# Hadamard stage of a fused kernel: feature groups paired on GpSimd, transform products half as wide, another order of copies

## The chip, the cores and the metric

The kernel runs on one core of one Trainium2 chip. The metric is device time in microseconds (us) of that core, the median of some runs; lower is better. The core has five engines with queues of their own, which run apart from each other and meet only at semaphores: TensorE (PE in the rows, its weight loads PEld), VectorE (DVE), ScalarE (ACT), GpSimd (POOL) and SyncE (SP).

## What is computed

Four layers follow each other on 1024 tokens of 256 features: a token-routed expert layer, a mixture of 16 experts, a latent attention and a ternary feed-forward layer. The change touches only the last one, which is cut here to what matters:

```
def h_bitlinear(x, w):
    return jnp.einsum('bsh,oh->bso', act_quant(fwht(x)), weight_quant(w))
gate = bitlinear(x, w_gate)          # 1024 features out
up = bitlinear(x, w_up)
intermediate = jax.nn.silu(gate) * up
return h_bitlinear(intermediate, w_down)

def act_quant(x, bits=8):            # per token
    scale = 128 / clip(max(abs(x)), 1e-5)
    return clip(round(x * scale), -128, 127) / scale
```

`fwht` is the Walsh-Hadamard transform over the 1024 features of a token. A feature number is a chunk number of three bits (8 chunks of 128) and a place in the chunk; the transform is the 128-point transform within each chunk, and then sums and differences of chunks, one bit of the chunk number at a time.

## The kernel before

The program is written engine by engine; the order on each engine is the order of the code, and there is no scheduler. The last layer works with **units**: unit v (0 to 15) is one chunk of features (v mod 8) of one half of the tokens (v // 8), a block of 128 features by 512 tokens. For each unit:

- TensorE, `products(v)` (L1460 to L1479): four matmuls of bf16, two for gate and two for up, into two of the PSUM banks 0 to 5.
- VectorE, `gate_b(v)` (L2162): gate times the tokens' scale, into `gt`.
- ScalarE, `silu_b(v)` (L999): silu of `gt` into `gsl`.
- VectorE, `up_b(v)` (L2170): `gsl` times up into `hp`, two buffers.
- ScalarE, `hi_b(v)`: a copy of `hp` rounded to fp32r, the high part, into `hpB_hi` or `hpA_hi` (B for the first half of the tokens, A for the second). The line is that of the helper `copy`, L700.
- GpSimd (L689): `hp` minus the high part, the low part, into `hpB_lo` or `hpA_lo`.

Ten units (`AHEAD`) run ahead of the transform. Units 0 to 3 lie beside the end of the attention, which also gives the last two token tiles: their variance goes to GpSimd for the power -0.5 (`power3`, L542), VectorE normalises and quantises them (`quantise`, L1591 and L2137 to L2146), TensorE turns them (L1079, L1458) and ScalarE copies them (`bits_x`, L993). Units 6 and 7 stand behind the turns, units 8 to 15 behind the copies.

Then eight **tiles** t of 128 tokens:

- TensorE, `transform(t)` (L1521): for each of two banks, 4 and 5, four matmuls with the high parts of four chunks and four with the low parts, each 512 columns wide. The moving operand `had` is the 128-point matrix four times side by side with signs, so that the sums over two bits of the chunk number are made in PSUM.
- ScalarE, `f_copy(t)` (L700, `f`): bank 5 into `f1`. VectorE, `butterfly(t)` (L2219, two instructions): bank 4 plus and minus `f1` into `F`, the third bit.
- VectorE, `feature_scale(t)` (L2225 to L2229): maximum and scale. ScalarE, `f_round(t)` (L1040). VectorE, `clip(t)` (L2233).
- TensorE, `turn_f(t)` (L1079, `F`): eight transposes into banks 6 and 7. ScalarE, `f_bits(t)` (L1048): two copies to `fqT`.
- TensorE, `final(t)` (L1545): eight matmuls. VectorE, `x4(t)` (L2237, L2239): the result added to `X`. SyncE stores it.

`transform(0)` to `transform(3)` need all of units 0 to 7, `transform(4)` to `transform(7)` all of units 8 to 15. Units 10 to 15 are made between the first tiles, two for each tile. `turn_f(1)` and `turn_f(2)` also wait for `x4(0)` and `x4(1)`, as `final(0)` and `final(1)` use bank 6.

Of the kernel before, what the change touches and what calls it, by code (L numbers as in the profile page):

```python
# [7 lines left out]
F32 = mybir.dt.float32  # L8
# [68 lines left out]
def build(nc, x_d, tok_d, seg_d, ctxT_d, router_d, gu_d, dn_d, kvc_d, dq_d, uq_d, uk_d, uv_d, qr_d, qrs_d,  # L77
# [6 lines left out]
    with ctx:  # L84
# [9 lines left out]
        def place(words, *groups):  # L94
# [3 lines left out]
            for n, group in enumerate(groups):  # L98
                scope = ExitStack()
                with scope:  # L100
                    for name, (shape, dt) in group.items():
# [96 lines left out]
                        "gt": ([P, 2, BANK], F32), "gsl": ([P, 2, BANK], F32), "hp": ([P, 2, BANK], F32),  # L198
                        "had": ([P, 4, 4, P], F32R), "f1": ([P, 2, BANK], F32), "F": ([P, 2, FI], F32)}))
# [38 lines left out]
        xqT, invB, diag, gt, gsl, hp, had, f1, F = [m[k] for k in "xqT invB diag gt gsl hp had f1 F".split()]  # L238
# [66 lines left out]
        (signs_a, x_scaled_v, x_rounded, xq_turned_p, xq_copied_a, diagonal_v, bit_scaled_v,  # L305
# [3 lines left out]
             "signs_a x_scaled_v x_rounded xq_turned_p xq_copied_a diagonal_v bit_scaled_v "  # L309
# [74 lines left out]
        def x_bank(t):  # L384

            return t % 2 if t < NT - TB else 6 + t % 2

# [151 lines left out]
        def _(pool):  # L539
# [144 lines left out]
            for v in range(2 * NF):  # L684
                if v == BESIDE - 1:
                    power3(NT - TB, TB)
                pool.wait_ge(hidden_high_a, UNITS + v + 1)
                n, c = divmod(v, NF)
                pool.tensor_tensor(hp_lo[n][:, c, :], hp[:, v % 2, :], hp_hi[n][:, c, :].bitcast(F32), ALU.subtract  # L689
                                   ).then_inc(bit_low_g, 1)  # L690
# [3 lines left out]
        def _(act):  # L694
# [286 lines left out]
            def signs():  # L981

                act.wait_ge(masked_v, 4 * PAIRS)
                for r in range(4):
                    for q in range(4):
                        e = act.activation(had[:, r, q, :], had1, ACT.Copy, scale=-1.0 if odd(r & q) else 1.0)
                e.then_inc(signs_a, 1)
# [9 lines left out]
            def silu_b(v):  # L997
                act.wait_ge(bit_scaled_v, v + 1)
                act.activation(gsl[:, v % 2, :], gt[:, v % 2, :], ACT.Silu, scale=bscale[:, 0:1]).then_inc(gate_silu_a, 1)  # L999

            def hi_b(v):
                n, c = divmod(v, NF)
                act.wait_ge(hidden_v, UNITS + v + 1)
                copy(hp_hi[n][:, c, :], hp[:, v % 2, :]).then_inc(hidden_high_a, 1)

            for i in range(SLOTS):
# [19 lines left out]
                if i == PAIRS + 4:  # L1026
                    for v in range(1, BESIDE):
                        silu_b(v)
                        hi_b(v - 1)


            def f_copy(t):
# [3 lines left out]
                copy(f1[:, t % 2, :], bank[5][:, :]).then_inc(transform_copied_a, 1)  # L1036
# [15 lines left out]
            for v in range(BESIDE, AHEAD):  # L1052
# [3 lines left out]
                hi_b(v - 1)  # L1056
# [3 lines left out]
            hi_b(AHEAD - 1)  # L1060
# [15 lines left out]
        def _(pe):  # L1076
# [383 lines left out]
            def products(v):  # L1460
                n, c = divmod(v, NF)
# [9 lines left out]
                for g in range(2):  # L1471
                    if before is not None:
                        pe.wait_ge((bit_scaled_v, hidden_v)[g], (0, UNITS)[g] + before + 1)
                    for k in range(KD):
                        w = slice(k * FI + c * P, k * FI + (c + 1) * P)
# [35 lines left out]
            def transform(t):  # L1511
                n, x = divmod(t, NT // 2)
                tile = slice(x * P, (x + 1) * P)
                for part, ready in ((hp_hi[n], hidden_high_a), (hp_lo[n], bit_low_g)):
                    pe.wait_ge(ready, (UNITS if ready is hidden_high_a else 0) + NF * (n + 1))
                    for z in range(2):
                        if t >= 1 and ready is hidden_high_a:
                            pe.wait_ge((butterfly_v, transform_copied_a)[z], (2 * t, t)[z])
                        for r in range(4):
                            m_ = had[:, r, :, :].rearrange("p q j -> p (q j)")  # L1520
# [841 lines left out]
```

## Time and profile before

| | us |
|---|---|
| median of 3 runs (579.54 to 583.58) | 580.24 |
| the profiled execution | 580.38 |
| its span (first to last event in the trace) | 578.6 |

The page gives the busy time over the span: TensorE 86%, VectorE 79%, ScalarE 61%, GpSimd 55%. The last layer's part of the span is its last 85 us, from about 494 us on; what lies before is the same in both kernels but for the names of a few lines. The profiled execution stands 0.14 us over the median, so its times may be used as they are; 1.78 us of it lie outside the span.

### The profile page before, as it was taken

What the parts mean: (1) busy time and instruction counts of PE and PEld (TensorE: products, weight loads), DVE (VectorE), ACT (ScalarE), POOL (GpSimd) and SP (SyncE); (2) the same over time, 40 slices, a digit from 0 to 9 for tenths busy, and PEclk for the clock granted to TensorE, in tenths of its full rate; (3) what the DMA queues carried; (4) which work ended last, traced back from release to release, by engine and by line L of the source; (5) the groups of instructions that cost most, each with busy time, mean ns of one, the idle gap of its engine ahead of it and who ended that gap; (6) DMA issues with size and microseconds to landing.
All of it is one profiled execution on the core that took longest, in us unless ns stands there. A gap on an engine that the chain in (4) does not pass through costs nothing.

```text
span 578.6 us, 11090 instructions
## 1 busy us (share of the span) xinstructions
PE 499.4 (86%) x3338; PEld 438.1 (76%) x3338; DVE 457.4 (79%) x1391; ACT 355.0 (61%) x909; POOL 316.9 (55%) x298
## 2 busy tenths in 40 slices
PE   0699979999899999995659999999899999588894
PEld 0488757878788898994449999999899998346673
DVE  4779956976879888856598889899989886769774
ACT  2344546343456675763247877878688889666643
POOL 2538671114358887315777787788577773363100
PEclk9989998999899999996598999999999999989997
DMA  8144444322363657745720100100000000000000
GB/s 277 39 125 127 131 152 119 87 55 64 106 185 111 198 141 212 163 128 146 281 56 19 29 19 19 29 18 2 2 1 2 2 2 2 0 1 10 10 28 27
DMA packets 27960, 45.24 MB, mean 78 GB/s; under 512 B 5696, under 2 KB 18848, under 8 KB 27264
## 3 DMA queue, kind: packets, MB, share of 16 engines
q1 hardware_dynamic: 21056, 28.15, 15.9%
q0 software_dynamic: 3792, 10.74, 7.7%
q10 hardware_dynamic: 3056, 5.65, 3.0%
q8 instruction: 29, 0.48, 0.3%
q14 instruction: 27, 0.22, 0.1%
HBM read 34.63 MB, written 8.85 MB: 75 GB/s over the span
## 4 chain that ended last, share of the span: by engine, by line
PE 52%; DVE 25%; issue 8%; ACT 6%; DMA 4%; POOL 4%; SPq 0%; DVEq 0%; ACTq 0%; POOLq 0%
PE bank L420 9%; PE bank L1079 8%; PE bank L422 8%; PE bank L421 8%; PE bank L1521 5%; PE bank L1281 2%; PE bank L1283 2%; PE bank L1282 2%; DVE pT_lo L1580 2%; DVE sc L2091 1%; ACT pr L955 1%; PE bank L1476 1%; DVE X L1632 1%; DMA seg<-seg_dram 1%; DVE yk L2025 1%
## 5 line engine op out<-in xcount | busy, mean ns | idle before, releaser
L589 POOL DMA_INDIRECT inb<-rows_kept,row_of x47 | 46.9, 999 | 36.7 <-PE bank L1079 18.8
L955 ACT ACTIVATE pr<-sc,smin 128x256 f32<-128x256 f32 x128 | 63.3, 503 | 0.0
L666 POOL TENSOR_TENSOR Q_lo<-Q,Q_hi 128x512 fp32r<-128x512 f32 x32 | 41.5, 1296 | 22.6 <-ACT Q_hi L700 22.1
L2091 DVE CUSTOM_DVE_ANT_0 sc<-bank,bias 128x256 f32<-128x256 f32 x128 | 46.4, 418 | 0.0
L653 POOL TENSOR_TENSOR pr<-pr,srec 128x512 f32<-128x512 f32 x32 | 33.3, 1041 | 21.6 <-DVE srec L2098 21.6
L1580 DVE TENSOR_TENSOR pT_lo<-bank,pT_hi 128x512 fp32r<-128x512 f32 x64 | 41.1, 683 | 5.0 <-ACT pT_hi L700 5.0
L700 ACT ACTIVATE pT_hi<-bank 128x512 fp32r<-128x512 f32 x64 | 35.0, 595 | 13.6 <-PE bank L1079 13.3
L660 POOL TENSOR_TENSOR Q<-Q,rot 128x512 f32<-128x512 f32 x32 | 41.1, 1285 | 0.0
L617 POOL DMA_INDIRECT yk<-slots_y,slot x32 | 33.3, 1039 | 13.8 <-issue 5.8
L1079 PE MATMUL bank<-const,pr 128*128 128x128 f32 x256 | 34.8, 279 | 6.5 <-POOL pr L653 6.5
L547 POOL TENSOR_TENSOR Wd<-wd_raw,Wd 128x512 fp32r<-128x512 f32 x13 | 16.8, 1292 | 43.1 <-ACT Wd L747 43.1
L964 ACT ACTIVATE pr<-pr,srec 128x256 f32<-128x256 f32 x64 | 29.1, 502 | 16.6 <-DVE srec L2098 16.6
L420 PE MATMUL bank<-pT_hi,V_hi 128*128 128x256 f32 x128 | 36.9, 288 | 2.7 <-DVE pT_lo L1580 2.7
L420 PE MATMUL bank<-K_hi,Q_hi 128*128 128x256 f32 x128 | 36.8, 288 | 0.0
L421 PE MATMUL bank<-K_lo,Q_hi 128*128 128x256 f32 x128 | 36.5, 285 | 0.0
L422 PE MATMUL bank<-K_hi,Q_lo 128*128 128x256 f32 x128 | 36.4, 285 | 0.0
L422 PE MATMUL bank<-pT_hi,V_lo 128*128 128x256 f32 x128 | 36.2, 283 | 0.0
L421 PE MATMUL bank<-pT_lo,V_hi 128*128 128x256 f32 x128 | 36.2, 283 | 0.0
L1079 PEld LDWEIGHTS bank<-const,pr 128*128 128x128 f32 x256 | 29.1, 143 | 8.7 <-issue 4.5
L547 POOL TENSOR_TENSOR Wg<-wg_raw,Wg 128x512 fp32r<-128x512 f32 x22 | 28.2, 1300 | 12.1 <-ACT Wg L700 12.1
L1281 PE MATMUL bank<-Wg,xT_hi 128*128 x94 | 31.2, 332 | 0.0
L542 POOL TENSOR_TENSOR rstd<-vare,mhalf 128x1 f32<-128x1 f32 (+3 forms) x26 | 17.0, 655 | 25.8 <-DVE vare L1667 8.0
(347 smaller groups left out, 1949.2 us busy)
## 6 DMA issues: line engine op xcount, KB each, us to landing
slots_y<-yb SPq DMA_DIRECT2D x47, 128.0 KB, 2.4
wg_raw<-gate_up_dram SPq DMA_DIRECT2D x22, 256.0 KB, 2.8
bw<-bits_dram ACTq DMA_DIRECT2D x3, 1024.0 KB, 6.3
wd_raw<-down_dram SPq DMA_DIRECT2D x16, 128.0 KB, 2.1
wo<-wo_dram SPq DMA_DIRECT2D x2, 1024.0 KB, 6.8
wd_raw<-down_dram SPq DMA_DIRECT2D x30, 64.0 KB, 2.2
gu_raw<-gate_up_dram SPq DMA_DIRECT2D x6, 256.0 KB, 3.6
X<-x_dram SPq DMA_DIRECT2D x2, 512.0 KB, 6.6
```

Source lines behind the costliest of these rows:

```text
L420: eng.matmul(out, w_hi, m_hi, start=first, stop=False, **kw)
L421: eng.matmul(out, w_hi, m_lo, start=False, stop=False, **kw)
L422: return eng.matmul(out, w_lo, m_hi, start=False, stop=last, **kw)
L547: return pool.tensor_tensor(out, in_, hi.bitcast(F32), ALU.subtract)
L589: pool.indirect_dma_start(inb[:, j % NIN, :], None, rows_d, bass.IndirectOffsetOnAxis(row_of[:, j:j + 1], 0)).then_inc(slots_in[j % NIN], 16)
L660: pool.tensor_tensor(Q[:, r, :], Q[:, r, :], rot[:, r, :, :].rearrange("p h s -> p (h s)"), ALU.add).then_inc(queries_summed_g, 1)
L666: pool.tensor_tensor(Q_lo[:, i % 2, :], Q[:, i % 2, :], Q_hi[:, i % 2, :].bitcast(F32), ALU.subtract).then_inc(queries_low_g, 1)
L955: e = act.activation(pr[:, i % 2, z, :], sc[:, i % 2, z, :], ACT.Exp, bias=smin[:, i % 2, z:z + 1], scale=-1.0, accum_out=ssum[:, i % 2, z ...
L1079: return pe.transpose(out, in_, ident)
L1281: pe.matmul(out, xT_hi[:, j % 3, k, :], hi, start=(k == 0), stop=False)
L1580: return dve.tensor_tensor(out, in_, hi.bitcast(F32), ALU.subtract)
L2091: dve.tensor_tensor_reduce(sc[:, r, z, :], bank[2 + h][:, u * S:(u + 1) * S], bias[:, TB * b_ + u, :], 1.0, 3.0e38, ALU.add, ALU.min, smin ...
```

## The change

- `transform(t)` now makes the 128-point transform and only one bit of the chunk number. It has as many matmuls, 16, each 256 columns wide in place of 512; `had` has four blocks in place of sixteen.
- The second bit is made ahead of the split: when two units v and v+1 (v even) lie in `hp`, which has four buffers now, GpSimd writes their sum and their difference into `sd` (`pair`, L705), two instructions more for each two units. High and low parts are taken of `sd`. The chunks are taken in another order (`chunk`), so that the right two follow each other.
- `silu_b` writes over `gt`, and `gsl` is gone; `gate_b(v)` waits for `up_b(v - 2)`.
- On ScalarE `hi_b` comes two units after `silu_b`; from the tiles on, `f_copy(t + 1)` and the `hi_b` of two units stand ahead of `f_round(t)`. On VectorE `butterfly(t + 1)` stands ahead of `clip(t)`, and `x4(t - 1)` at the end of tile t. `feature_scale` has one instruction less.
- Tiles 4 and 6 use banks 2 and 3 for the transform, and on TensorE `transform(t + 1)` stands ahead of `turn_f(t - 1)` from tile 5 on.

```
-            for v in range(2 * NF):
-                if v == BESIDE - 1:
+            def pair(v, op):
+                if v >= 2:
+                    pool.wait_ge(bit_low_g, v - 1)
+                return pool.tensor_tensor(sd[:, v % 2, :], hp[:, v % 4 // 2 * 2, :], hp[:, v % 4 // 2 * 2 + 1, :], op).then_inc(pair_g, 1)
+            def lo_b(v):
+                pool.wait_ge(hidden_high_a, UNITS + v + 1)
...
+            for v in range(0, 2 * NF, 2):
+                if v == BESIDE - 2:
                     power3(NT - TB, TB)
+                pool.wait_ge(hidden_v, UNITS + v + 2)
+                pair(v, ALU.add)
+                pair(v + 1, ALU.subtract)
+                lo_b(v)
+                lo_b(v + 1)
...
             def hi_b(v):
-                act.wait_ge(hidden_v, UNITS + v + 1)
-                copy(hp_hi[n][:, c, :], hp[:, v % 2, :]).then_inc(hidden_high_a, 1)
+                act.wait_ge(pair_g, v + 1)
+                copy(hp_hi[v // NF][:, part_of(v), :], sd[:, v % 2, :]).then_inc(hidden_high_a, 1)
...
             for t in range(NT + 1):
                 if t >= 1:
                     f_bits(t - 1)
+                if t + 1 < NT and t + 1 != NT // 2:
+                    f_copy(t + 1)
+                for v in range(AHEAD + 2 * t - 2, AHEAD + 2 * t):
+                    if v < 2 * NF:
+                        hi_b(v)
+                if t + 1 == NT // 2:
+                    f_copy(t + 1)
                 if t < NT:
                     f_round(t)
                 for v in units_after(t):
                     silu_b(v)
-                if t + 1 < NT:
-                    f_copy(t + 1)
-                for v in units_after(t):
-                    hi_b(v)
...
-                        for r in range(4):
-                            m_ = had[:, r, :, :].rearrange("p q j -> p (q j)")
-                            e = pe.matmul(bank[4 + z][:, :], part[:, 4 * z + r, tile], m_,
-                                          start=(r == 0 and ready is hidden_high_a), stop=(r == 3 and ready is bit_low_g))
+                    for k in range(2):
+                        out = bank[transform_bank(t) + z][:, k * D:(k + 1) * D]
+                        for y, part in enumerate((hp_hi[n], hp_lo[n])):
+                            for r in range(2):
+                                e = pe.matmul(out, part[:, 4 * z + 2 * k + r, tile],
+                                              had[:, r, :, :].rearrange("p q j -> p (q j)"),
+                                              start=(y == 0 and r == 0), stop=(y == 1 and r == 1))
...
-            for t in range(NT + 2):
-                if t < NT:
-                    butterfly(t)
-                if t >= 2:
-                    x4(t - 2)
+            butterfly(0)
+            for t in range(NT + 1):
                 if t < NT:
                     feature_scale(t)
                 for v in units_after(t):
                     gate_b(v)
+                if t + 1 < NT:
+                    butterfly(t + 1)
                 if t < NT:
                     clip(t)
                 for v in units_after(t):
                     up_b(v)
+                if t >= 1:
+                    x4(t - 1)
```

Three places where the order on an engine matters. First **GpSimd**, from the first unit to the end of the first half of the tokens, before and then after (L689 and L710 are the low part, L705 the sum and the difference, L542 and L559 the power for the last two token tiles):

```order
L689 TENSOR_TENSOR hpB_lo<-hp,hpB_hi 128x512 [waits hidden_high_a] x3
L542 TENSOR_TENSOR rstd<-vare,mhalf 128x2 [waits variance_v]
L689 TENSOR_TENSOR hpB_lo<-hp,hpB_hi 128x512 [waits hidden_high_a] x5
```

```order
L705 TENSOR_TENSOR sd<-hp 128x512 x2
L710 TENSOR_TENSOR hpB_lo<-sd,hpB_hi 128x512 x2
L559 TENSOR_TENSOR rstd<-vare,mhalf 128x2
L705 TENSOR_TENSOR sd<-hp 128x512 x2
L710 TENSOR_TENSOR hpB_lo<-sd,hpB_hi 128x512 x2
```

The power stands behind four instructions where it stood behind three, and each further two units bring four where they brought two; the last two rows come three times.

Second **ScalarE**, from the first `f_copy` (L700 and L730, `f`) to the second `f_round` (L1040 and L1069), before and then after:

```order
L700 ACTIVATE f<-bank 128x512 [waits transform_p]
L1040 ACTIVATE F<-F,const,fs 128x1024 [waits feature_scale_v]
L999 ACTIVATE gsl<-gt,bscale 128x512 [waits bit_scaled_v] x2
L700 ACTIVATE f<-bank 128x512 [waits transform_p]
L700 ACTIVATE hpA_hi<-hp 128x512 [waits hidden_v] x2
L1048 ACTIVATE fqT<-bank,const 128x512 [waits feature_turned_p] x2
L1040 ACTIVATE F<-F,const,fs 128x1024 [waits feature_scale_v]
```

```order
L730 ACTIVATE f<-bank 128x512 [waits transform_p] x2
L730 ACTIVATE hpA_hi<-sd 128x512 [waits pair_g] x2
L1069 ACTIVATE F<-F,const,fs 128x1024 [waits feature_scale_v]
L1028 ACTIVATE gt<-gt,bscale 128x512 [waits bit_scaled_v] x2
L1077 ACTIVATE fqT<-bank,const 128x512 [waits feature_turned_p] x2
L730 ACTIVATE f<-bank 128x512 [waits butterfly_v,transform_p]
L730 ACTIVATE hpA_hi<-sd 128x512 [waits pair_g] x2
L1069 ACTIVATE F<-F,const,fs 128x1024 [waits feature_scale_v]
```

The rounding of a tile stood ahead of the next tile's `f_copy`, and now stands behind it and behind two `hi_b`.

Third **VectorE**, in the second tile, before and then after:

```order
L2219 TENSOR_TENSOR F<-bank,f 128x512 [waits transform_copied_a]
L2225 TENSOR_REDUCE fm<-F 128x1 [waits butterfly_v]
L2162 TENSOR_TENSOR gt<-bank,invB 128x512 [waits gate_silu_a,xq_copied_a,gate_p] x2
L2233 TENSOR_SCALAR F<-F 128x1024 [waits feature_rounded_a]
L2170 TENSOR_TENSOR hp<-gsl,bank 128x512 [waits bit_low_g,gate_silu_a,up_p] x2
```

```order
L2265 TENSOR_REDUCE fm<-F 128x1 [waits butterfly_v]
L2202 TENSOR_TENSOR gt<-bank,invB 128x512 [waits hidden_v,xq_copied_a,gate_p] x2
L2259 TENSOR_TENSOR F<-bank,f 128x512 [waits feature_turned_p,transform_copied_a]
L2273 TENSOR_SCALAR F<-F 128x1024 [waits feature_rounded_a]
L2210 TENSOR_TENSOR hp<-gt,bank 128x512 [waits pair_g,gate_silu_a,up_p] x2
```

The butterfly of the next tile stands ahead of this tile's clip.

## Rows read from the trace of the kernel before

**Rows 1.** Two stretches: busy time (instructions) of PE, PEld, DVE, ACT, POOL; granted clock
```profile
520.00:530.00 10.00, 9.56 (x46) 7.16 (x47) 9.54 (x20) 6.51 (x10) 2.54 (x2) 1.00 0.00 1
550.00:560.00 10.00, 9.66 (x58) 7.78 (x57) 6.87 (x17) 4.95 (x6) 0.00 (x0) 1.00 0.08 26
```

**Rows 2.** The chain that ended last, from 478 us on: start, length, what
```profile
478.39 0.12 PE bank L422
...
514.34 3.67 PE bank L1521 x16
518.03 0.60 ACT f L700
519.98 1.23 DVE fm L2225
522.07 1.25 ACT F L1040
525.36 0.87 PE bank L1079 x8
526.24 0.86 PE bank L1476 x4
530.77 0.89 PE bank L1545 x8
540.29 1.81 issue
546.86 0.61 ACT f L700
```

**Rows 3.** Groups by line and shape, 480 to 579 us: busy, mean ns, idle before
```profile
L999 ACT ACTIVATE gsl<-gt,bscale 128x512 f32<-128x512 f32 x16 | 11.2, 718 | 6.7 <-DVE gt L2162 6.7
L2219 DVE TENSOR_TENSOR F<-bank,f 128x512 f32<-128x512 f32 x16 | 10.3, 684 | 5.4 <-ACT f L700 5.1
L1048 ACT ACTIVATE fqT<-bank,const 128x512 bf16<-128x512 f32 x16 | 10.2, 683 | 8.0 <-PE bank L1079 7.9
L689 POOL TENSOR_TENSOR hpA_lo<-hp,hpA_hi 128x512 fp32r<-128x512 f32 x8 | 10.1, 1282 | 18.2 <-ACT hpA_hi L700 18.2
L700 ACT ACTIVATE hpA_hi<-hp 128x512 fp32r<-128x512 f32 x8 | 4.7, 619 | 0.3 <-DVE hp L2170 0.3
L2239 DVE SCALAR_TENSOR_TENSOR X<-bank,fo,X 128x256 f32<-128x256 f32 x8 | 3.9, 483 | 3.8 <-PE bank L1545 3.5
```

**Rows 4.** Timeline of GpSimd: start, length, instruction, idle before and its releaser
```profile
500.55 0.72 POOL L542 TENSOR_TENSOR rstd<-vare,mhalf 128x2 f32<-128x2 f32 x1 [0.17 <-DVE vare L2251]
507.01 2.51 POOL L689 TENSOR_TENSOR hpB_lo<-hp,hpB_hi 128x512 fp32r<-128x512 f32 x2 [5.74 <-ACT hpB_hi L700]
513.58 1.28 POOL L689 TENSOR_TENSOR hpB_lo<-hp,hpB_hi 128x512 fp32r<-128x512 f32 x1 [0.27 <-ACT hpB_hi L700]
```

**Rows 5.** Timeline of VectorE, 496 us to the end
```profile
496.03 0.68 DVE L2170 TENSOR_TENSOR hp<-gsl,bank 128x512 f32<-128x512 f32 x1
504.97 0.69 DVE L2162 TENSOR_TENSOR gt<-bank,invB 128x512 f32<-128x512 f32 x1
570.64 0.69 DVE L2233 TENSOR_SCALAR F<-F 128x1024 f32<-128x1024 f32 x1 [1.31 <-ACT F L1040]
```

**Rows 6.** TensorE by stretch: busy (instructions), granted clock
```profile
499.00:503.50 4.50, 0.04 (x1) 1.00 0.00 0
504.70:510.30 5.60, 5.35 (x16) 0.50 0.00 0
```

**Rows 7.** The chain where the granted clock is 0.50, at 283 us
```profile
283.28 0.21 PE bank L420
```

**Rows 8.** Timelines of VectorE and GpSimd at 304 us, of VectorE at 439 us
```profile
304.20 1.15 DVE L1591 TENSOR_SCALAR hn<-X,mv,rstd 128x256 f32<-128x256 f32 x1
303.93 1.27 POOL L660 TENSOR_TENSOR Q<-Q,rot 128x512 f32<-128x512 f32 x1
...
439.18 0.40 DVE L1591 TENSOR_SCALAR xr<-X,mv,rstd 128x256 f32<-128x256 f32 x1
```

More of the change, by code:

```diff
@@ L386, in x_bank, with chunk, part_of, transform_bank @@
             return t % 2 if t < NT - TB else 6 + t % 2
+        def chunk(v):
+            z, c0 = divmod(v % NF // 2, 2)
+            return 4 * z + 2 * (v % 2) + c0
+        def part_of(v):
+            z, c0 = divmod(v % NF // 2, 2)
+            return 4 * z + 2 * (v % 2) + c0
+        def transform_bank(t):
+            return 2 if t >= 4 and t % 2 == 0 else 4
+        def last_transform(t):
+            return max((w for w in range(t) if transform_bank(w) == transform_bank(t)), default=None)
         def final_bank(t):
@@ L983, in signs @@
                 act.wait_ge(masked_v, 4 * PAIRS)
-                for r in range(4):
-                    for q in range(4):
-                        e = act.activation(had[:, r, q, :], had1, ACT.Copy, scale=-1.0 if odd(r & q) else 1.0)
-                e.then_inc(signs_a, 1)
+                for r in range(2):
+                    for q in range(2):
+                        act.activation(had[:, r, q, :], had1, ACT.Copy, scale=-1.0 if r and q else 1.0)
             def bits_x(t):
@@ L1055, in _ @@
                 silu_b(v)
-                hi_b(v - 1)
+                hi_b(v - 2)
                 if v == LATE_TURN:
@@ L1512, in transform @@
                 n, x = divmod(t, NT // 2)
[L1513 to L1519, printed above, removed]
[L1520 to L1524 removed]
+                tile, w = slice(x * P, (x + 1) * P), last_transform(t)
+                pe.wait_ge(hidden_high_a, UNITS + NF * (n + 1))
+                pe.wait_ge(bit_low_g, NF * (n + 1))
+                if t == 4:
+                    pe.wait_ge(hidden_v, UNITS + 2 * NF)
+                for z in range(2):
+                    if w is not None:
+                        pe.wait_ge((butterfly_v, transform_copied_a)[z], (2 * (w + 1), w + 1)[z])
+                    for k in range(2):
+                        out = bank[transform_bank(t) + z][:, k * D:(k + 1) * D]
+                        for y, part in enumerate((hp_hi[n], hp_lo[n])):
+                            for r in range(2):
+                                e = pe.matmul(out, part[:, 4 * z + 2 * k + r, tile],
+                                              had[:, r, :, :].rearrange("p q j -> p (q j)"),
+                                              start=(y == 0 and r == 0), stop=(y == 1 and r == 1))
+                    e.then_inc(transform_p, 1)
             def turn_f(t):
@@ L1553, in _ @@
                 products(v)
-            pe.wait_ge(signs_a, 1)
             pe.wait_ge(xq_copied_a, 2 * NT)
-            for t in range(NT + 2):
-                if t < NT:
-                    transform(t)
+            for t in range(3):
+                transform(t)
                 if t >= 2:
                     final(t - 2)
-                for v in units_after(t)[:1]:
-                    products(v)
-                if 1 <= t <= NT:
+                products(AHEAD + 2 * t)
+                if t >= 1:
                     turn_f(t - 1)
-                for v in units_after(t)[1:]:
-                    products(v)
+                products(AHEAD + 2 * t + 1)
+            transform(3)
+            for t in range(3, NT + 2):
+                final(t - 2)
+                if NT // 2 < t + 1 < NT:
+                    transform(t + 1)
+                if t <= NT:
+                    turn_f(t - 1)
+                if t + 1 == NT // 2:
+                    transform(t + 1)
         @block.vector
@@ L2252, in _ @@
                               ).then_inc(variance_v, TB)
+            up_b(BESIDE - 1)
             for v in range(BESIDE, AHEAD):
```

56 lines of the change are left out of this document (26 added, 30 removed).

## The prediction

> **What bounds the kernel now.** I read the stretches first, then the chain, then the groups and timelines of the last 85 us. Between the first tiles TensorE and VectorE are both full (9.56 and 9.54 of 10 us), and GpSimd works 2.54 of 10; when the units are done only TensorE is full (9.66) [rows 1]. The chain says the same: its largest pieces are the 16 matmuls of a transform, 3.67 us each time, and from the first `f_copy` at 518.03 to the fifth at 546.86 it lies mostly on TensorE [rows 2]. So the transform is the right thing to cut, in two kinds of place: where TensorE alone is full, each us cut counts; between tiles 0 and 4 VectorE is as full, and there the order of the engines decides. GpSimd looks free: in the groups its low parts waited 18.2 us for ScalarE's high parts [rows 3]. But that is free time only if work is there early, and the low parts of half of the units gate a transform each. The question is when the units can be ready now.
>
> The sum goes by four landmarks of the profiled execution: first `f_copy` 518.03, fifth `f_copy` 546.86, last clip 570.64, end of span 578.6; 1.78 us lie outside the span.
>
> **The transform.** 16 matmuls in both kernels, 256 columns in place of 512. Back to back, 256 columns take 0.12 us in the attention [rows 2], so 16 x 0.12 = 1.92 us, against 3.67: 1.75 less, 14.0 over eight tiles. That is what the change can bring at most. Should the weight loads not keep up, it would be less; in that attention row each matmul has its own load too, so I take 1.92.
>
> **Step 1, units 0 to 7 (to the first `f_copy`).** GpSimd has the pairs to make: inputs of fp32, 128x512, two operands in SBUF, as `Q<-Q,rot`, 1.27 us [rows 8], and the low parts are 2.51 for two [rows 4]. I take 1.26 for each, 5.05 for two units against 2.5.
> - The first pair starts when unit 1 lies in `hp` at 496.7 [rows 5] and takes until 501.9. Behind it stands the power for the last two token tiles, done at 502.65; before, it was done at 501.27 [rows 4]. Cost 1.4 us: from there to `gate_b(4)` is one chain on VectorE (3.7 us, to 504.97 [rows 5]), so that comes at 506.35.
> - Now `hi_b(2)` stands behind `silu_b(4)` on ScalarE: 506.35 + 0.7 (gate) + 0.65 (silu) + 0.6 (high) + gaps = 508.4. Only then the low part of unit 2 can start. GpSimd then has, up to the low part of unit 7, ten instructions, 12.6 us, and waits 0.5 for `hi_b(5)`, which stands behind the copies of `bits_x`. It ends at 521.5, where before it ended at 514.86 [rows 4]. The transform, 1.92, follows: first `f_copy` at 523.45, **+5.4**. Nothing covers this: TensorE can do products 8 and 9 in that time, and no more. Before, the products 8 and 9 and not the low parts ended last here.
>
> **Step 2, tiles 0 to 3 with units 8 to 15 (first to fifth `f_copy`, before 28.8).** The new order makes a ring of waits, which I follow round once from `f_copy(t+1)`: copy 0.57, two `hi_b` 1.14 (they stand between), `f_round` 1.25, clip 0.69, `up_b` 0.68, then the second half of the products 0.43, `turn_f` 0.87, the next products 0.86, the next transform 1.92, gaps 0.2: **8.6 us** a tile [rows 2, 3, 5]. Each is in the queue of its engine behind the one before or waits for it: the rounding now stands behind the next tile's copy, and that tile's transform behind this tile's turn. Before, the rounding waited for nothing of the next tile, and VectorE's own work set the pace: butterfly 1.3, scale 2.1 (519.98 to 522.07), two gates 1.3, clip 0.7, two `up_b` 1.3, some 6.6, and 0.65 for `x4` [rows 2, 3]. In numbers:
> - first to second `f_copy`: copy 0.6, butterfly 1.3, transform 1.92, gaps: 3.9.
> - second to third: 8.6.
> - third to fourth: `turn_f(1)` waits for `x4(0)`, which now stands at the end of the tile, behind both `up_b`: 0.8 more, 9.4. (This wait stood in the old chain as "issue", 1.81 us [rows 2], for `x4(1)`.)
> - fourth to fifth: copy 0.57, two `hi_b` 1.14, round 1.25, clip 0.69, two `up_b` 1.3; then GpSimd's four instructions for units 14 and 15, 5.05, with 0.45 for `hi_b(14)` behind `f_bits(2)`; the transform 1.92, gaps 0.15: 12.5.
> Sum 34.4, **+5.6**. Fifth `f_copy` at 557.85.
>
> **Step 3, tiles 4 to 7.** Here the cut comes through, with two pairs of banks. Fifth `f_copy` to the end of clip 4: `final(2)` 0.89 and transform 1.92 from the same moment on, half a turn 0.45, `f_bits` 1.25, copy 0.6, butterfly 1.3, clip 0.7: 7.1. Then a ring of `f_bits` 1.25, `final` 0.89, transform 1.92 and half a turn, 4.6 a tile (VectorE: scale 1.87, butterfly 1.3, clip 0.7, `x4` 0.65, so 4.5), twice; 4.5 for the last, which has no transform beside it. From the end of the last clip to the end nothing changes: 571.34 to 578.6, 7.26 [rows 5]. Sum 28.1 against 31.74: **-3.6**.
>
> With nothing else that is 557.85 + 28.1 = 585.95, +1.78 = **587.7**, 7.3 over the profiled execution. The removed instruction of the scale (0.18) is in it; the signs (16 to 4 copies) lie in ScalarE's idle time and count nothing.
>
> **Two things that the walk leaves out, both from rows.**
> - *VectorE held by GpSimd.* A `TENSOR_SCALAR` of VectorE that started while GpSimd was in a two-operand instruction took 1.15 us and ended 0.15 after it, where 0.40 is usual [rows 8]. The normalisation of the last tokens now starts as GpSimd begins a pair (+1.05), and the clips 0 to 2 start while it has 0.75 us of low parts to go, since these begin with the same `hi_b` after which the rounding runs (3 x 0.75). Sum **+3.3**. (The other end is 0, if the clip gets in first; by the one row that shows the case I give the term 3 chances in 4.) The page "SBUF — State Buffer" of the Trainium skill, section "Who interferes with whom", says the same as the row: the two share a port pair, the loser is blocked for the whole instruction. By its rule the time would be that with the 3.3 us, 591.0 without the term that follows; the page says also that issue order decides, so each of the four places may fall out.
> - *TensorE's clock.* After TensorE idled from 499 us the granted clock fell, and the next 5.6 us, in which it was busy for 5.35, ran at 0.50, the lower of its levels, 1.2 GHz [rows 6]; there 256 columns take 0.21 us [rows 7]. Now it idles some 5.5 us before transform 0 and some 4 us before transform 4. Each then takes 3.4 in place of 1.92, +1.5; products 10 and 11 after the one +0.6, `final(2)` and transform 5 after the other +1.3. Sum **+4.9**.
>
> Forecast: 587.7 + 3.3 + 4.9 = 595.9, so **596.0**.
>
> **The rivals.**
> 1. *The ring is no ring, VectorE paces tiles 0 to 3* (no clear gain or loss). If the ring's parts overlap more than I read, VectorE's work is the floor: from the first `f_copy` 0.6, then 1.3 + 6.4 + 7.0 + 6.4 to `up_b(15)`, 5.05 of GpSimd, transform 1.92, so 28.7 in place of 34.4: 582.0, and up to 585.3 with the held instructions. For it: VectorE was the pace before [rows 1]. Against it: each link is a wait or a place in a queue.
> 2. *The cut comes through* (faster). GpSimd alone sets the pace: 521.5, then 16 x 1.26 = 20.2 for units 8 to 15, transform 1.92, step 3 28.1, +1.78: 573.5. It decides if units 8 to 15 come at 2.5 us each; then the fifth `f_copy` would come at 543.6, 3.3 sooner than now. Against it: two units come with each tile, and a tile costs VectorE 6.4 to 7.0, not 5.
> 3. *The clock falls within the ring too* (slower still). TensorE idles some 4 us of each round between the first half of the products and `up_b`. If the 4.1 us of matmuls behind it run at the lower clock, the two full rounds get 4.1 longer each, 604 in all; if half of them do, 600.
>
> That the edit does not do what it says is excluded by the order of the instructions, which shows the narrow matmuls and the added ones.
>
> **How the numbers follow.** 1% (5.8 us, 574.4 to 586.0) is about what a measurement of this kernel can tell from no change. My walk, with all, some or none of the two added terms, and rival 3: 0.82, all slower by over 1%. Rival 1 and other reasons for a small difference: 0.12. Rival 2: 0.06. The likeliest is the walk with both terms, 596. The range takes in the bare walk (587.7), the upper end of rival 1 (585.3) and rival 3: 585 to 604. Left out are rival 2, most of rival 1 and a ring wholly at the lower clock with more behind it, under 0.2 together.
>
> **What the profile of the changed kernel would show.** Step 1: GpSimd without gaps from about 509 to 522 us, first `f_copy` at 523 to 526. Step 2: distances of the `f_copy` of 4, 8.6 to 10, 9.4 to 11 and 12.5 to 15 us; TensorE idle some 4 us in each; GpSimd's last low part just ahead of transform 4. Step 3: clips 4.5 us apart. The held instructions: normalisation and clips longer than 0.41 and 0.69 us. It is wrong if the roundings do not follow the second `hi_b` of a tile at once, or if transform 0 starts before 518.

## The result, and the profile after

The changed kernel takes **600.28 us** (595.5 to 601.81, 4 runs) where the kernel before took 580.35 beside it: a ratio of 1.0332, 95% interval [1.0295, 1.0369]. The profiled execution took 599.32, its span is 597.5, and 1.8 us lie outside as before. So the forecast of 596.0 was right in direction and 4 us short; the range 585 to 604 holds the result.

The starts of the eight `f_copy` are the ruler here. These are the first five, from the timeline of ScalarE of the changed kernel (start, length, instruction, idle before and its releaser); the others start at 573.24, 578.00 and 582.75:

```profile
524.31 0.60 ACT L730 ACTIVATE f<-bank 128x512 f32<-128x512 f32 x1 [4.65 <-PE bank L1556]
528.66 0.60 ACT L730 ACTIVATE f<-bank 128x512 f32<-128x512 f32 x1 [3.75 <-PE bank L1556]
540.53 0.60 ACT L730 ACTIVATE f<-bank 128x512 f32<-128x512 f32 x1 [3.51 <-PE bank L1556]
551.91 0.60 ACT L730 ACTIVATE f<-bank 128x512 f32<-128x512 f32 x1 [2.54 <-PE bank L1556]
567.72 0.60 ACT L730 ACTIVATE f<-bank 128x512 f32<-128x512 f32 x1 [5.94 <-PE bank L1556]
```

Where step 1 begins has to be chosen with care. GpSimd's power stands behind the first pair now, so its start already holds a part of the cost. VectorE's instruction ahead of it, which writes the variance of the last two token tiles (`vare`), is a better mark: the pairs do not stand ahead of it. In the kernel before, and then in the changed kernel with the power behind it:

```profile
500.21 0.19 DVE L2251 TENSOR_SCALAR vare<-mv 128x2 f32<-128x2 f32 x1
```
```profile
498.20 0.58 DVE L2291 TENSOR_SCALAR vare<-mv 128x2 f32<-128x2 f32 x1
499.94 0.72 POOL L559 TENSOR_TENSOR rstd<-vare,mhalf 128x2 f32<-128x2 f32 x1
```

With 518.03 and 546.86 of before [rows 2] and the span of 578.6, the steps of the prediction read:

| | before | after | change | forecast, all terms in |
|---|---|---|---|---|
| up to `vare` | 500.21 | 498.20 | -2.0 | 0 |
| step 1, from there to the first `f_copy` | 17.82 | 26.11 | +8.3 | +8.0 |
| step 2, first to fifth `f_copy` | 28.83 | 43.41 | +14.6 | +10.0 |
| step 3, fifth to the end | 31.74 | 29.78 | -2.0 | -2.3 |

(The forecast's terms put by step: 5.4 + 1.05 + 1.5; 5.6 + 2.25 + 0.6 + 1.5; -3.6 + 1.3.) Of the first row the change can explain 0.3 us (before, an `up_b` ahead of `vare` waited 0.32 for a low part, and now there are four buffers). The rest is how executions differ: `vare` starts at 496.30 to 500.21 us in the traces of this document, and the kernel before with some matmuls added (`before_idle_work`) has it at 496.44. So from `vare` on the change costs 20.9 us in this execution, where the forecast has 15.6.

The chain of waits (start, length, what) shows the ring link by link, here from the third `f_copy`:

```profile
540.53 0.60 ACT f L730
541.13 1.04 ACT hpA_hi L730 x2
542.16 1.13 ACT F L1069
543.29 1.23 ACT gt L1028 x2
...
544.71 0.66 DVE hp L2210
...
545.42 0.60 PE bank L1507 x2
546.02 0.68 issue
546.70 1.94 PE bank L1110 x8
548.64 1.33 PE bank L1507 x4
549.97 1.92 PE bank L1556 x16
...
558.08 1.96 PE bank L1110 x8
...
560.65 1.15 ACT hpA_hi L730 x2
561.79 2.13 issue
563.93 3.76 PE bank L1556 x16
```

Three things are to be seen. The links and their order are those that the prediction follows, but for the clip, on which more below. The issue of 0.68 is the wait for `x4(0)`. And TensorE's links are long: eight turns take 1.94 us where they took 0.87 [rows 2], the transform of tile 4 (at 563.93) 3.76 where that at 549.97 takes 1.92. The stretches say why. Compare with [rows 1], where TensorE was busy for 9.56 us of 520 to 530 at clock 1.00 (columns as there):

```profile
532.50:538.90 6.40, 5.35 (x20) 3.90 (x21) 4.60 (x9) 1.53 (x3) 2.50 (x2) 0.50 0.00 1
556.40:569.90 13.50, 7.92 (x36) 7.05 (x37) 4.81 (x11) 4.13 (x6) 4.98 (x4) 0.50 0.03 10
```

Each round of the ring leaves TensorE idle, and the granted clock then stands at 0.50, the level of 1.2 GHz, for a part of the matmuls behind.

Then there is VectorE held by GpSimd. The timelines of VectorE, ScalarE and GpSimd (the timeline merges what follows at once, so 2.61 is two instructions of 1.34 each, 0.41 before):

```profile
500.69 2.61 DVE L1631 TENSOR_SCALAR hn<-X,mv,rstd 128x256 f32<-128x256 f32 x2 [1.32 <-POOL rstd L559]
531.46 1.44 DVE L2273 TENSOR_SCALAR F<-F 128x1024 f32<-128x1024 f32 x1 [0.88 <-ACT F L1069]
532.82 1.27 DVE L2210 TENSOR_TENSOR hp<-gt,bank 128x512 f32<-128x512 f32 x2
...
531.33 1.32 ACT L1028 ACTIVATE gt<-gt,bscale 128x512 f32<-128x512 f32 x2
```
```profile
500.63 2.53 POOL L705 TENSOR_TENSOR sd<-hp 128x512 f32<-128x512 f32 x2
508.28 2.50 POOL L710 TENSOR_TENSOR hpB_lo<-sd,hpB_hi 128x512 fp32r<-128x512 f32 x2 [5.12 <-ACT hpB_hi L730]
...
529.86 2.49 POOL L710 TENSOR_TENSOR hpA_lo<-sd,hpA_hi 128x512 fp32r<-128x512 f32 x2 [6.28 <-ACT hpA_hi L730]
```

The clips beside low parts take 1.44 us, those beside an idle GpSimd 0.69, as before [rows 5]. The first of the two normalisations waits for the sum, the second for the difference. The hold of a clip lies on the path, though the chain puts this link down to ScalarE's silus (1.23). The first `up_b` needs only the first of the two silus, which ends at about 532.0, yet starts at 532.82, as the clip ends. In the run `order_both`, described below, a clip that is not held shows the difference; there the silus run from 531.08 to 532.40, and the first `up_b` starts 0.67 us after the clip in place of 1.36:

```profile
531.20 0.69 DVE L2271 TENSOR_SCALAR F<-F 128x1024 f32<-128x1024 f32 x1
531.87 1.30 DVE L2208 TENSOR_TENSOR hp<-gt,bank 128x512 f32<-128x512 f32 x2
```

### The profile page after: what moved, and what is told of

Its sections match the earlier page's. It is cut to its first block, busy times and chain, and to the rows that moved or that the text cites. A ratio compares the mean times of both kernels' runs of the same rounds, so it can differ in the third digit from the quotient of the medians.

```text
span 597.5 us, 11093 instructions
## 1 busy us (share of the span) xinstructions
PE 494.8 (83%) x3338; PEld 435.4 (73%) x3338; DVE 461.3 (77%) x1383; ACT 351.8 (59%) x897; POOL 336.9 (56%) x314
## 4 chain that ended last, share of the span: by engine, by line
PE 46%; DVE 26%; issue 10%; ACT 7%; POOL 6%; DMA 4%; SPq 1%; DVEq 0%; ACTq 0%; POOLq 0%
PE bank L1110 9%; PE bank L437 7%; PE bank L438 7%; PE bank L439 7%; PE bank L1556 3%; PE bank L1312 2%; PE bank L1314 2%; PE bank L1313 2%; DVE pT_lo L1620 2%; DVE sc L2131 1%; ACT pr L985 1%; PE bank L1507 1%; POOL hpB_lo L710 1%; DVE X L1672 1%; POOL sd L705 1%
## 5 line engine op out<-in xcount | busy, mean ns | idle before, releaser
L606 POOL DMA_INDIRECT inb<-rows_kept,row_of x47 | 47.1, 1003 | 35.1 <-PE bank L1110 19.3
L730 ACT ACTIVATE pT_hi<-bank 128x512 fp32r<-128x512 f32 x64 | 35.0, 595 | 13.6 <-PE bank L1110 13.3
L634 POOL DMA_INDIRECT yk<-slots_y,slot x32 | 33.3, 1040 | 14.4 <-issue 5.7
L1110 PE MATMUL bank<-const,pr 128*128 128x128 f32 x256 | 34.8, 280 | 5.9 <-POOL pr L670 5.8
L1507 PE MATMUL bank<-xqT,bits 128*128 128x512 bf16 x64 | 21.7, 481 | 12.8 <-DVE hp L2210 9.0
L559 POOL TENSOR_TENSOR rstd<-vare,mhalf 128x1 f32<-128x1 f32 (+3 forms) x26 | 17.1, 659 | 25.9 <-DVE vare L1707 8.2
```

Of the source, the lines that this page charges most:

```text
L606: pool.indirect_dma_start(inb[:, j % NIN, :], None, rows_d, bass.IndirectOffsetOnAxis(row_of[:, j:j + 1], 0)).then_inc(slots_in[j % NIN], 16)
L730: return act.activation(out, in_, ACT.Copy)
L1110: return pe.transpose(out, in_, ident)
```

## Experiments

Three things changed together: the pairs on GpSimd, the order on ScalarE and VectorE, and, through them, TensorE's clock. The first runs take one away each. Step 1 is read in each run from the start of `vare` to the first `f_copy`: 17.8 us before, 26.1 after.

### The order of copies, undone engine by engine

On ScalarE (`order_act`), on VectorE (`order_dve`), and on both (`order_both`):

```
# order_act
-                if t + 1 < NT and t + 1 != NT // 2:
-                    f_copy(t + 1)
                 for v in range(AHEAD + 2 * t - 2, AHEAD + 2 * t):
                     if v < 2 * NF:
                         hi_b(v)
-                if t + 1 == NT // 2:
-                    f_copy(t + 1)
                 if t < NT:
                     f_round(t)
                 for v in units_after(t):
                     silu_b(v)
+                if t + 1 < NT:
+                    f_copy(t + 1)
# order_dve
-            butterfly(0)
-            for t in range(NT + 1):
+            for t in range(NT + 2):
+                if t < NT:
+                    butterfly(t)
+                if t >= 2:
+                    x4(t - 2)
                 if t < NT:
                     feature_scale(t)
                 for v in units_after(t):
                     gate_b(v)
-                if t + 1 < NT:
-                    butterfly(t + 1)
                 if t < NT:
                     clip(t)
                 for v in units_after(t):
                     up_b(v)
-                if t >= 1:
-                    x4(t - 1)
```

> The changed kernel with ScalarE's order in the tiles undone: the two hi_b, then f_round(t), the silus, and f_copy(t + 1) last. Theory (a ring of waits through f_copy, hi_b, f_round and, on VectorE, butterfly ahead of clip): only a part of the ring is gone, since clip(t) still stands behind butterfly(t + 1) and that needs the same copy. Each round loses 1.14 (hi_b) + 1.25 (round) and gains 1.3 (butterfly), so 1.1 less, three times, and the clips are no longer held by GpSimd (3 x 0.75): 600.3 - 3.3 - 2.3 = 594.7. Rival (ScalarE's order alone makes the delay): the distances of the f_copy fall to VectorE's 6.6 to 7.3 us, 586 or below. Rival (GpSimd's load alone makes it): 600, no change.

> The changed kernel with VectorE's order in the tiles undone: clip(t) ahead of butterfly(t + 1), x4 at its old place. Theory (ring): the ring runs on through f_copy(t + 1), hi_b and f_round(t), all as long as before; only the 0.8 us that turn_f(1) waited for x4(0) goes: 599.5, within 1% of 600.3. Rival (VectorE's order alone makes the delay): 586 or below.

> Both orders undone, on ScalarE and VectorE; all else as in the changed kernel, pairs and narrow transform too. Theory (ring): only now is it cut. VectorE's work sets the pace from the first to the fifth f_copy, 28.7 us where 43.4 were measured, so 600.3 - 14.7 = 585.6 by that, and TensorE idles less, so that its clock falls less often; step 1 stays late: 583 to 588. Rival (GpSimd's load alone): 597 to 600. Rival (the clock alone, whatever the order): 595 or above.

Measured: `order_act` 599.78 (1.0343 [1.0315, 1.0371]), `order_dve` 605.19 (1.0449 [1.0391, 1.0507]), `order_both` 594.85 (1.0245 [1.0206, 1.0283]). All three came out slower than expected, by 5.1, 5.7 and 9.3 us (the last against 585.6). Only both orders together gain on the changed kernel: each half leaves a ring, through ScalarE or through the butterfly that stands ahead of the clip. With `order_act` the rounds took 9.9 and 9.9 us, but the last tiles 6.15 each in place of 4.8, since the next `f_copy` stands behind the rounding: in its trace step 2 gained 4.3 us and step 3 lost 2.5 of them. `order_dve` puts `x4` later, and `turn_f(1)` and `turn_f(2)` wait 1.45 and 3.12 us for it.

`order_both` shows what the prediction's rival 1 describes, for two rounds, in the timeline of ScalarE:

```profile
526.02 0.60 ACT L730 ACTIVATE f<-bank 128x512 f32<-128x512 f32 x1 [4.29 <-PE bank L1554]
532.30 0.58 ACT L730 ACTIVATE f<-bank 128x512 f32<-128x512 f32 x1
538.73 0.58 ACT L730 ACTIVATE f<-bank 128x512 f32<-128x512 f32 x1
547.92 0.58 ACT L730 ACTIVATE f<-bank 128x512 f32<-128x512 f32 x1
560.83 0.60 ACT L730 ACTIVATE f<-bank 128x512 f32<-128x512 f32 x1 [4.82 <-PE bank L1554]
```

6.3 and 6.4 us are VectorE's own pace. The third round is 9.2: its chain has 1.88 of wait for `x4(0)`, 1.96 for turns at the lower clock, and the high parts behind `f_bits`, ahead of the rounding. The fourth is 12.9. So the ring made by the new order is real (11.9 and 11.4 against 6.4 and 9.2), but it is not all of step 2, which takes 34.8 us here and not the 28.7 of VectorE's work. Step 3 takes 31.8 in place of 29.8, for the reason given for `order_act`. By its time alone the run would fit the rival "the clock alone, whatever the order" (595 or above); it is the two rounds of 6.3 and 6.4 us that speak against it.

### The pairs, taken out

`no_pairs` leaves out the sums and differences of units, and so one bit of the transform; all else stands as in the changed kernel. `no_pairs_order` undoes both orders as well.

```
-                pool.wait_ge(hidden_v, UNITS + v + 2)
-                pair(v, ALU.add)
-                pair(v + 1, ALU.subtract)
                 lo_b(v)
                 lo_b(v + 1)
...
-                act.wait_ge(pair_g, v + 1)
-                copy(hp_hi[v // NF][:, part_of(v), :], sd[:, v % 2, :]).then_inc(hidden_high_a, 1)
+                act.wait_ge(hidden_v, UNITS + v + 1)
+                copy(hp_hi[v // NF][:, part_of(v), :], hp[:, v % 4, :]).then_inc(hidden_high_a, 1)
```

> The changed kernel without the sums and differences of pairs: high and low parts are taken of hp itself, so one bit of the transform is left out of the computation. Orders as in the changed kernel. Theory (two causes): step 1 becomes short, the first f_copy comes at about 517 where it came at 524.3 (-7), and behind unit 15 only two GpSimd instructions stand (-2.5), but the ring stays at 10 to 12 us a round: 600.3 - 9.5 = 591. Rival (GpSimd's load is all of it): the fifth f_copy comes at 545, 577 in all. Rival (ring is all of it): 598 to 600.

> Both orders undone and the pairs left out (one bit of the transform is not computed). What the pairs cost once the ring is cut. Theory (with the ring cut GpSimd's sums and differences were what ended last in tiles 2 and 3, 9.2 and 12.9 us against 6.3 and 6.4, and in step 1): step 1 gives 6.5 as in the run without pairs, tiles 2 and 3 some 3 more: 594.9 - 9.5 = 585.4, still slower than the kernel before. Rival (hi_b ahead of f_round and TensorE's clock make tiles 2 and 3 long, not the pairs): only the 6.5 of step 1, 588.4.

Measured: 593.74 (1.0223 [1.0182, 1.0263]) and 587.27 (1.0122 [1.0052, 1.0191]). In `no_pairs` step 1 takes 20.6 us (497.45 to 518.07) in place of 26.1, so 5.5 of the 8.3 that step 1 lost are GpSimd's added instructions. Of these 1.4 come at its very start: the power starts 1.74 us behind the start of `vare` in the changed kernel, 0.36 in `no_pairs`. The four distances behind it are 4.7, 12.0, 11.5 and 15.8, the same as with pairs (4.35, 11.9, 11.4, 15.8): **in the ring the pairs cost nothing** (the low parts, beside which the clips are held, stand in both kernels). That the last leg stays at 15.8 was no part of my walk, which had put 5.05 us of GpSimd on it. `no_pairs_order` came nearer to the rival of its expectation: tiles 2 and 3 are long (9.7 and 11.7) without pairs too. Its step 2 takes 34.1 us, 5.3 more than in the kernel before, with neither the ring nor the pairs. Its rival names two causes, `hi_b` ahead of the rounding and TensorE's clock; no run takes them apart.

### The held normalisation

`pair_held` makes the second pair wait until the last tokens are normalised (the last diagonals written).

```
+                if v == BESIDE - 2:
+                    pool.wait_ge(diagonal_v, NT)
                 pair(v, ALU.add)
```

> The changed kernel, but GpSimd takes up the second pair (units 2 and 3) only when the diagonals of the last tokens are made. It does the same work, later. Theory (VectorE's normalisation, 2.61 us in place of 0.73, stood still while GpSimd made this pair): it takes 0.73 again and the first low part behind it starts 1.6 us sooner; 600.3 - 1.6 = 598.7. Rival (the 2.61 has nothing to do with GpSimd's pair): it stays at 2.61 and the time rises by up to 2.5.

Measured: 598.70 (1.0329 [1.0253, 1.0404]), which the interval can't tell from the changed kernel. The trace can: step 1 took 25.1 in place of 26.1. The timelines of VectorE and GpSimd:

```profile
499.43 0.73 DVE L1633 TENSOR_SCALAR hn<-X,mv,rstd 128x256 f32<-128x256 f32 x2 [1.32 <-POOL rstd L559]
503.06 2.51 POOL L705 TENSOR_TENSOR sd<-hp 128x512 f32<-128x512 f32 x2 [3.66 <-issue]
```

With GpSimd idle the same two instructions take 0.73 us, so 1.88 of their 2.61 came from it. That is the case that the page "SBUF — State Buffer" of the Trainium skill, section "Who interferes with whom", describes: the loser is blocked for the whole instruction.

### The clock

`fill_idle` gives TensorE matmuls whose results nobody reads, in its idle times: 6 ahead of transform 0, 12 between the halves of products 12 and of products 14, 8 ahead of transform 4.

```
+            def idle_work(bk, n):
+                for _ in range(n):
+                    pe.matmul(bk[:, :], bits[:, 0, 0:P], xqT[:, 0, 0:HALF], start=True, stop=True)
...
+                    if g == 1 and v in (12, 14):
+                        if v == 14:
+                            pe.wait_ge(feature_bits_a, 2)
+                        idle_work(bank[7], 12)
```

> The changed kernel with matmuls without use where TensorE idles: 6 ahead of transform 0, 12 each between the two halves of products 12 and 14, 8 ahead of transform 4. Nothing waits for them but TensorE's own next instruction. Theory (the granted clock falls with these idle times and makes turns, products and transforms behind them up to twice as long; in the trace about 1.0 at transform 0, 2.5 in each of two rounds, 1.0 at turn 2, 1.85 at transform 4 and 1.2 behind it): with more than half of it won back, 593 to 596. Rival (the clock is not on the path): 600 or more, by the matmuls added.

Measured: 591.06 (1.0174 [1.0103, 1.0245]), 9.2 us less than the changed kernel by work added. The chain of waits of `fill_idle`, one round:

```profile
527.67 0.60 ACT f L730
528.27 1.04 ACT hpA_hi L730 x2
529.30 1.13 ACT F L1069
530.43 1.23 ACT gt L1028 x2
...
531.85 0.69 DVE hp L2221
...
532.58 0.60 PE bank L1511 x2
533.18 0.87 PE bank L1110 x8
534.06 0.86 PE bank L1511 x4
534.92 1.92 PE bank L1564 x16
```

and its stretches, whose granted clock is to be compared with the changed kernel's 0.50:

```profile
532.50:538.90 6.40, 6.32 (x45) 4.90 (x46) 4.82 (x10) 3.31 (x6) 3.36 (x3) 1.00 0.01 4
```

The round sums to 9.2 us, the next to 10.05. The prediction had 8.6 + 0.75 = 9.35 and 9.4 + 0.75 = 10.15 for them: at full clock the ring has the size that was worked out. What the changed kernel shows above it (11.9 and 11.4) is the clock: 4.0 us in the two rounds, where all of TensorE's part at the lower clock would have been 8.2. So rival 3 was true for about half of it. How much falls under the lower clock changes from run to run: with the same order in the tiles, the rounds took 10.8 and 11.1 us in `pair_held`.

### The last leg

The chain of the changed kernel runs over `turn_f(2)`, `f_bits(2)` and only then the high parts of units 14 and 15. `hi_first` puts these two copies ahead of `f_bits(2)`, and `no_pairs_hi_first` does the same in `no_pairs`.

```
+                if t + 1 == NT // 2:
+                    hi_b(2 * NF - 2)
+                    hi_b(2 * NF - 1)
                 if t >= 1:
                     f_bits(t - 1)
```

> The changed kernel with one move on ScalarE: the high parts of units 14 and 15 stand ahead of f_bits(2) and not behind it. Theory (the last leg's path, fourth to fifth f_copy, runs over turn_f(2), f_bits(2), then the high parts): the high parts start as each sum is there, 558.7 and 560.0 in the changed kernel's times, the low parts end at 562.5 in place of 563.9, the leg takes 14.4 us in place of 15.8, the time is 598.9. Rival (the leg is set by GpSimd's four instructions and nothing else): it stays at 15.8, 600.3. The rounds before, 11.9 and 11.4, do not change by either.

> The changed kernel without the sums and differences of units (one bit of the transform is left out) and with the same move. Theory: in no_pairs both units lie ready at 551.7 and ScalarE is free, but the high parts start at 555.0, behind f_bits(2). Ahead of it they start by 551.7, the low parts end at 554.2, and transform 4 starts behind turn_f(2) at 554.4 in place of 558.25: the leg takes 12.0 us in place of 15.8, the time is 590. So the pairs would then cost 2.4 us of this leg, which the order of the copies hides. Rival: no_pairs' leg of 15.8 has another cause; it stays, 593.7.

Measured: 596.87 (1.0291 [1.0236, 1.0347]) and 588.08 (1.015 [1.0094, 1.0206]). The leg itself, fourth to fifth `f_copy`, in the timelines of ScalarE, of the one and of the other:

```profile
551.53 0.60 ACT L730 ACTIVATE f<-bank 128x512 f32<-128x512 f32 x1 [2.52 <-PE bank L1559]
565.87 0.60 ACT L730 ACTIVATE f<-bank 128x512 f32<-128x512 f32 x1 [4.51 <-PE bank L1559]
```
```profile
544.36 0.60 ACT L727 ACTIVATE f<-bank 128x512 f32<-128x512 f32 x1 [3.42 <-PE bank L1556]
556.33 0.60 ACT L727 ACTIVATE f<-bank 128x512 f32<-128x512 f32 x1 [3.12 <-PE bank L1556]
```

14.3 and 12.0 us, where 14.4 and 12.0 were expected. So the place of two copies set this leg, and hid 2.4 us of GpSimd's pairs. The times fell by more than the legs did, 3.4 us in place of 1.4 and 5.7 in place of 3.8; in both traces step 3 is 1.0 us shorter too, which was not forecast.

### A version of both

The runs say where each part pays. GpSimd's pairs cost in step 1 and the new order in the rings, while step 3 gains. `half_pairs` is the kernel before with pairs and the narrow transform for units 8 to 15 and tiles 4 to 7 alone. The old order stands up to tile 3, the new one from tile 4 on, and from unit 12 on the high parts stand ahead of `f_bits`.

```
# GpSimd
+            for v in range(NF, 2 * NF, 2):
+                pool.wait_ge(hidden_v, UNITS + v + 2)
+                for w, op in ((v, ALU.add), (v + 1, ALU.subtract)):
...
+                lo_b(v)
+                lo_b(v + 1)
# ScalarE, for each tile t
+                if t >= 2:
+                    for v in made:
+                        hi_b(v)
                 if t >= 1:
                     f_bits(t - 1)
# TensorE
             def transform(t):
+                if t >= NT // 2:
+                    return narrow(t)
```

> The kernel before, with the change in its second half only: units 0 to 7 without pairs and with the wide transform, units 8 to 15 with pairs on GpSimd and the narrow transform in two pairs of banks; orders as before up to tile 3, as in the changed kernel from tile 4 on; the hi_b of units 8 to 15 stand in ScalarE's idle time. Theory (the pairs cost in step 1 and through the ring, not in GpSimd's idle time of tiles 0 to 3): first f_copy as in the kernel before, fifth 0.8 sooner (narrow transform -1.75, pairs +0.9), step 3 28.7 in place of 31.7: 580.9 - 3.8 = 577.1. Rival (pairs hold up VectorE and GpSimd in tiles 0 to 3 as well): 580 or above.

Measured: **577.22** (10 runs), 0.9938 [0.9904, 0.9972] to the kernel before: it beats both, the kernel before by 0.6%. Its timeline of ScalarE:

```profile
517.95 0.60 ACT L724 ACTIVATE f<-bank 128x512 f32<-128x512 f32 x1 [4.13 <-PE bank L1577]
...
539.98 0.60 ACT L724 ACTIVATE f<-bank 128x512 f32<-128x512 f32 x1 [0.84 <-PE bank L1577]
547.23 0.60 ACT L724 ACTIVATE f<-bank 128x512 f32<-128x512 f32 x1 [0.99 <-PE bank L1560]
```

Step 2 takes 29.3 us (28.8 before) though GpSimd has 17.6 us of work in it, and step 3 28.1 (575.3 - 547.23; 31.74 before): the whole gain of the cut at a price of 0.5 us. The time met its expectation, though not by the sum that stands there: from `vare` to the fifth `f_copy` this trace has 48.5 us where the kernel before has 46.7, not 0.8 less. Step 1 took 19.3 us (from 498.69) in place of 17.8, as the clock was low in front of transform 0, which took 4.74 us in place of 3.67; before, 512 to 514.3 us ran at 1.00:

```profile
511.00:514.00 3.00, 2.83 (x9) 1.71 (x10) 1.49 (x4) 1.52 (x3) 1.87 (x2) 0.66 0.00 0
```

So this trace lies 3.3 us below that of the kernel before, as the medians do, but only 1.8 of it come from `vare` on; the other 1.5 lie ahead, where the two kernels are the same but for the buffers of `hp`.

In this trace TensorE is idle up to 503.3 us, and the first products of the last tokens run at clock 0.50. Two more runs tried matmuls of no use there (22) and ahead of the last turn (8), in `half_pairs` and in the kernel before.

```
# TensorE
+                    pe.wait_ge(x_after3_v, NT)
+                    idle_work(bank[7], 22)
...
+                if t == NT:
+                    pe.wait_ge(butterfly_v, 2 * NT)
+                    idle_work(bank[2], 8)
```

> half_pairs with TensorE kept at work by matmuls of no use into the spare bank: 22 ahead of the last tokens' turns, 8 ahead of the last tile's turn. Theory (the low clock of the last layer's start lies on the path): half_pairs shows TensorE idle from about 498 to 503 us and a granted clock of 0.50 from 501.7 to 508.5 while it works for the first Hadamard product. At twice the clock 1.5 to 2.5 us of that come back before the first copy of features, and 0.6 to 1 us at the last tile; time 574 to 575, ratio to half_pairs 0.995. Rival (VectorE's row of clips and groups sets that stretch, not TensorE): the time stays at 577.2, or rises by up to 1 us where the added matmuls stand ahead of the real ones.

> The kernel before with the same matmuls of no use at the same two places and nothing else. Theory: the same gain as in half_pairs, 2 to 3 us: 577.5 to 578.5, ratio 0.995 to 0.997. Then the added matmuls and not the pairs are what is worth having, and half_pairs_idle_work should lie below it by the 3 us that half_pairs lies below the kernel before. Rival: 580.5, no difference.

Measured: 578.02 (0.9968 [0.9936, 1.0001]) and 579.38 (1.001 [0.9976, 1.0044]): the rivals were right, no gain. Two stretches of `half_pairs_idle_work`:

```profile
503.00:510.00 7.00, 3.67 (x19) 1.58 (x18) 6.04 (x14) 5.04 (x11) 3.72 (x3) 0.96 0.00 0
510.00:516.00 6.00, 4.40 (x11) 2.12 (x11) 2.99 (x5) 2.74 (x5) 2.55 (x3) 0.50 0.01 3
```

The clock held through products 6 and 7 and fell behind them instead, for products 8 and 9 and the start of transform 0: the low clock had only moved, to where it lies on the path. In `before_idle_work` step 1 took 19.9 us (516.32 - 496.44) in place of 17.8, its products 8 and 9 and the start of transform 0 being at the lower clock, while the last tile, from the eighth `f_copy` on, gained 1.05 (12.7 in place of 13.8).

## Why the prediction was right, and where it was short

- **The sum.** 596.0 against a median of 600.28, inside the range. The layer itself grew by more than this says, 20.9 us from `vare` on against 15.6, and what lies ahead was 2.0 shorter in the profiled execution, nearly all of it by chance. Steps 1 and 3 came within 0.3 us of their sums; the 4.6 that are missing lie in step 2.
- **What bounds the kernel.** Right: the cut counts where TensorE alone is full. Step 3 fell by 2.0 us in the changed kernel, with a low clock at its start and end, and by 3.7 in `half_pairs`, where the term had 3.6. 28.1 was the walk's sum for the step, and `half_pairs` shows it.
- **Step 1.** Right. GpSimd ran almost without a gap from 508.28 (row above) to 521.1 us, and the first `f_copy` came at 524.31, in the span named. The step grew by 8.3 us from `vare` on, forecast 8.0, and the power came 1.4 later, as forecast. The pairs are 5.5 of it by `no_pairs`. The other 2.8, the later copies and the low clock, no run separates.
- **Normalisation held by GpSimd.** Right in kind, mis-sized: +1.05 was for one instruction held for the rest of one of GpSimd's. Both were held, each beside one of the pair: +1.88. By `pair_held` about 1.0 of it reaches the first `f_copy`.
- **Clips held.** As forecast, 0.75 each, 1.44 for 0.69, and on the path in full: the first `up_b` starts 1.36 us after the clip where it starts 0.67 after one that is not held. `fill_idle`'s rounds include it.
- **The ring.** Its links are right and at full clock its size too (9.2 and 10.05 against 9.35 and 10.15). The step that failed is the clock term: the sum took +4.9 us for four places at the edges of step 2 and left the rounds to rival 3. The four places were sized well (transform 0 took 3.02 us for 3.4, transform 4 3.76 for 3.4). In fact the clock fell in each round, 2.5 and 1.2 us more than forecast. Rival 3 was priced at 600 for half of the matmuls at the lower clock, which is what came; it should have been the forecast, as the walk itself gave TensorE 4 us of idle time a round, about the idle time in [rows 6] after which the clock fell.
- **The last leg.** Wrong in its path though near in its size (15.8 against 12.5 + 0.75 + 1.5). The walk put GpSimd's four instructions behind `up_b(15)`. The chain goes over `turn_f(2)` and `f_bits(2)`, both ahead of the high parts. The prediction names `f_bits(2)`, with 0.45 us, but takes it to start early; `turn_f(2)` waits for `x4(1)` and then takes 1.96 at the lower clock.
- **Rival 1** needs both orders undone, and then holds for two rounds only. **Rival 2** would have needed units at 2.5 us each; the rounds took 11.4 and more.

## What to carry to other kernels

Before an order of instructions is written for several engines at once, follow each new neighbour once round: a copy that stands between an engine and its next input closes a ring, and then no engine is full and the matmul time saved there is worth nothing. Where such a ring leaves TensorE idle, add the lower clock to the forecast at once, not as a rival. And split a change by stage: the same change lost 22.9 us up to the fifth `f_copy` and gained 2.0 to 3.7 behind it. To compare two traces stage by stage, start at an instruction that waits for nothing of the change.

## Unexpected of the hardware

- Added matmuls whose results nobody reads made the changed kernel 9.2 us faster. At the start of the layer, in the kernel before and in `half_pairs`, they bought nothing: the granted clock of 0.50 came 5 us later instead, on the path.
- A `TENSOR_SCALAR` of VectorE was held in six places of the changed kernel where GpSimd was in a two-operand instruction: 1.34 us for 0.41 (twice in a row), 1.44 for 0.69 (three clips), 0.58 for 0.19 (`vare`, of two elements a partition). A `TENSOR_REDUCE` of 128x1024 that started at 546.52, while GpSimd was in a sum (from 546.03), took its usual 1.21. The butterfly at 529.29, which reads PSUM and starts ahead of low parts that run from 529.86, took its usual 1.29 for two. Between two of GpSimd's that follow at once, one of VectorE's got in: the two normalisations took their turns with the sum and the difference, and GpSimd's two took 2.53 us, no longer than alone.
